# A fused decoder layer: the cross stage's maxima added by VectorE, two score tiles in one exp, outputs by halves, and a new table of priorities

## The reference

```python
x = _layernorm(x + self_attention(x))         # q, k, v: rope(x @ w.T) @ in_proj.T + b; softmax with causal mask
x = _layernorm(x + cross_attention(x, ctx))   # q = rope(x @ Wq.T + bq), k = rope(ctx @ Wk.T + bk), v = ctx @ Wv.T + bv
probs = softmax(x @ wg.T); top 2 of 8, weights normalised
out = sum over experts e of w_e * (silu(x @ w1[e].T) * (x @ w3[e].T)) @ w2[e].T
x = _layernorm(x + out)
```

## Time and profile before

| | us |
|---|---|
| median of 3 runs (249.85 to 252.05) | 249.91 |
| the profiled execution | 248.22 |
| its span, first to last instruction | 246.40 |
| PE busy (share of the span) | 232.7 (94%) |
| DVE busy | 186.0 (75%) |
| ACT busy | 161.3 (65%) |
| POOL busy | 89.1 (36%) |
| the chain of waits that ended last | PE 80%, DVE 10%, ACT 4%, issue 3%, DMA 2% |

### The profile page before, as it was taken

How to read it: one execution, slowest core, us unless ns; L and a number is a source line. 1 busy time by engine, 2 the same in 40 slices (tenths; PEclk the granted TensorE clock), 3 DMA queues, 4 the chain that set the end, 5 groups by cost and what they waited for, 6 DMA issues and landing times.

```text
span 246.4 us, 4685 instructions
## 1 busy us (share of the span) xinstructions
PE 232.7 (94%) x1438; PEld 164.7 (67%) x1438; DVE 186.0 (75%) x631; ACT 161.3 (65%) x332; POOL 89.1 (36%) x161
## 2 busy tenths in 40 slices
PE   7999999999999999999999999988899999999981
PEld 3456668666666776677765576553588878987860
DVE  5558987989879899986876898990399763348974
ACT  2488785889778779897898734747368765022234
POOL 9998547241432453355221211174011000470300
PEclk9999999999999999999999999999999999999998
DMA  6990002000003100000221000011311101010101
GB/s 237 340 330 3 1 1 85 3 1 4 0 0 117 56 1 3 1 0 3 81 87 60 32 1 3 0 53 58 106 32 44 45 21 54 25 53 11 39 7 43
DMA packets 10568, 12.57 MB, mean 51 GB/s; under 512 B 1200, under 2 KB 7728, under 8 KB 10416
## 3 DMA queue, kind: packets, MB, share of 16 engines
q1 hardware_dynamic: 9456, 10.43, 12.9%
q0 software_dynamic: 512, 1.05, 1.4%
q10 hardware_dynamic: 576, 0.79, 0.9%
HBM read 9.25 MB, written 3.01 MB: 50 GB/s over the span
## 4 chain that ended last, share of the span: by engine, by line
PE 80%; DVE 10%; ACT 4%; issue 3%; DMA 2%; DVEq 0%; ACTq 0%; SPq 0%
PE psB L1083 12%; PE psA L1054 12%; PE psO L1106 10%; PE psJ L952 3%; PE psJ L1186 3%; PE psJ L990 3%; PE psJ L953 3%; PE psJ L1067 2%; PE psA L1249 2%; PE psO L1111 2%; PE psO L982 2%; PE psJ L1065 2%; PE psA L1231 2%; PE psJ L997 1%; DMA xT<-xt_dram 1%
## 5 line engine op out<-in xcount | busy, mean ns | idle before, releaser
L1576 DVE CUSTOM_DVE_ANT_0 junk<-psA,c 128x128 bf16<-128x128 f32 (+3 forms) x128 | 55.7, 487 | 8.8 <-PE psA L1054 8.4
L1348 ACT ACTIVATE prob<-psB 128x512 f32<-128x512 f32 (+1 forms) x88 | 47.4, 558 | 13.6 <-PE psB L1083 11.8
L1083 PE MATMUL psB<-qb,kst 128*128 128x512 f32 (+3 forms) x128 | 38.0, 338 | 0.2 <-ACT prob_more L1348 0.2
L1054 PE MATMUL psA<-kst,qa 128*128 128x512 f32 (+1 forms) x88 | 36.6, 425 | 0.0
L1083 PEld LDWEIGHTS psB<-qb,kst 128*128 128x128 f32 x128 | 22.8, 189 | 11.4 <-issue 4.3
L1581 DVE TENSOR_REDUCE negm<-psA 128x3 f32<-128x462 f32 (+1 forms) x48 | 26.4, 579 | 4.5 <-PE psA L1054 3.9
L1348 ACT ACTIVATE prob_more<-psB 128x512 f32<-128x512 f32 (+1 forms) x48 | 24.5, 527 | 6.1 <-PE psB L1083 5.9
L1392 ACT ACTIVATE silu<-psA 128x512 f32<-128x512 f32 x16 | 9.6, 599 | 24.4 <-DVE hid L1739 18.0
L899 POOL TENSOR_SCALAR_AFFINE_SELECT prob<-prob 128x256 f32<-128x256 f32 x32 | 13.0, 408 | 31.3 <-ACT prob_more L1348 31.3
L1054 PEld LDWEIGHTS psA<-kst,qa 128*128 128x128 f32 x88 | 16.4, 188 | 6.0 <-issue 3.9
L1106 PE MATMUL psO<-prob_more,v 128*32 128x512 f32 (+3 forms) x128 | 20.3, 439 | 0.0
(11 more groups left out here) (198 smaller groups left out, 562.6 us busy)
## 6 DMA issues: line engine op xcount, KB each, us to landing
c<-w_dram SPq DMA_DIRECT2D x8, 256.0 KB, 2.6
w<-w_dram SPq DMA_DIRECT2D x1, 1024.0 KB, 4.7
xs_dram<-kst SPq DMA_DIRECT2D x1, 960.0 KB, 7.2
ys_dram<-ys SPq DMA_DIRECT2D x7, 128.0 KB, 1.8
rest<-xs_dram SPq DMA_DIRECT2D x3, 256.0 KB, 2.8
c<-c_dram SPq DMA_DIRECT2D x1, 666.0 KB, 8.5
xT<-xt_dram SPq DMA_DIRECT2D x2, 256.0 KB, 4.7
x_tok<-x_dram SPq DMA_DIRECT2D x1, 512.0 KB, 9.5
```

The source lines that it names most:

```text
L1054: last = nc.tensor.matmul(ps[:, c:c + heads * width].rearrange("p (n w) -> p n w", n=heads), qa[:, u % SLOTS, 128 * i:128 * i + 128], keys ...
L1083: last = nc.tensor.matmul(ps[:, c:c + S - 128 * kt], keys, qb[:, u % 2, 128 * kt:S], start=m == 0, stop=m == len(blocks) - 1, skip_group_c ...
L1348: nc.scalar.activation(dst, psB[n % SIZE["B"]][:, 0:cols], ACT.Exp, scale=SCALE).then_inc(b_done[n % SIZE["B"]], 1)
L1576: last = nc.vector.tensor_tensor_reduce(out=junk[:, p, cols], in0=psA[p][:, cols], in1=c32[:, C_MASK + S - width:C_MASK + S], scale=-1.0, ...
```

## The change

It has four parts.

1. In the cross stage (units 8 to 15, `max_by_dve`) MT no longer copies the q stack through the identity: PE only transposes the four blocks of `mpad` into the bank, and DVE adds `qa` to it on the way into `qb` (a new DVE item MT). ACT's copy is gone. The ring slot of `qa` is free only after DVE's addition.
2. In the self stage key tile 2 of two heads shares a bank (columns 0 and 256), and one exp of 512 columns takes both: 10 fills and 10 exps in a unit for 12.
3. The second pair of a batch row (p = 1, 3, 5, 7) is transposed and divided by halves (`turns`): OT becomes two jobs of two transposes, one reciprocal and two multiplications each on half the elements. ONT of half h waits for that half alone.
4. The table `EARLY` is another one, and the whole order with it. (Two waits are also written out more fully: DVE's OT waits for both ONT of the row before, and CQ waits for the low part too.)

```diff
+def max_by_dve(u):
+    st, b, g = unit(u)
+    return st == 1
 def b_fills(u):
     if unit(u)[0] == 0:
-        kinds = (((0, 0),), ((1, 0), (3, S - 128)), ((2, 0),))
-        return [tuple((kt, j, c) for kt, c in tiles) for tiles in kinds for j in range(G)]
+        kinds = (((0, 0),), ((1, 0), (3, S - 128)))
+        return [tuple((kt, j, c) for kt, c in tiles) for tiles in kinds for j in range(G)] + [((2, j, 0), (2, j + 1, 256)) for j in range(0, G, 2)]
+def turns(p):
+    return [("OT", (p, h)) for h in range(2)] if p % 2 else [("OT", (p,))]
...
-        add("MT", (u,), [("PE", 0.67), ("ACT", 0.5)], [("MP", (u,))],
+        add("MT", (u,), [("PE", 0.45), ("DVE", 0.69)] if max_by_dve(u) else [("PE", 0.67), ("ACT", 0.5)], [("MP", (u,))],
...
-            add("ONT", (st, b, h), [("PE", 0.24), ("ACT", 0.3)], [("OT", (p,))],
+            add("ONT", (st, b, h), [("PE", 0.24), ("ACT", 0.3)], [("OT", (p, h)), ("OT", (p - 1,))],
...
 EARLY = {
-    ('A', 11): 2, ('A', 13): 11, ('A', 14): -6, ('A', 7): -28, ('A', 8): 284, ('B', 1): 194, ('B', 13): 61, ('B', 6): 38,
+    ('A', 5): -39, ('A', 6): -17, ('A', 7): -199, ('B', 2): -11, ('B', 4): -19, ('B', 6): -55, ('B', 8): -30, ('CK',): -203,
...
                 elif kind == "MT":            # TensorE
-                    nc.tensor.matmul(ps[:, :], fr_id[:, :], qa[:, u % SLOTS, :], start=True, stop=False, skip_group_check=True)
+                    alone = max_by_dve(u)
+                    if not alone:
+                        nc.tensor.matmul(ps[:, :], fr_id[:, :], qa[:, u % SLOTS, :], start=True, stop=False, skip_group_check=True)
                     for i in range(QT):
-                        last = nc.tensor.matmul(ps[:, 128 * i:128 * i + 128], mpad[:, u % 2, i, :], fr_id[:, :], start=False,
-                                                stop=i == QT - 1, skip_group_check=True)
+                        last = nc.tensor.matmul(ps[:, 128 * i:128 * i + 128], mpad[:, u % 2, i, :], fr_id[:, :], start=alone,
+                                                stop=alone or i == QT - 1, skip_group_check=True)
...
+                elif kind == "MT":            # VectorE
+                    u, = args
+                    ps = bank(JOB[item])
+                    if u >= 2:
+                        dve.wait_ge(s_b, FILL["B"]["B", (u - 2, len(b_fills(u - 2)) - 1)] + 1)
+                    free(JOB[item], nc.vector.tensor_tensor(qb[:, u % 2, :], ps[:, :], qa[:, u % SLOTS, :].bitcast(FP32), ALU.add))
...
-                    nc.scalar.activation(dst, psB[n % SIZE["B"]][:, 0:cols], ACT.Exp, scale=SCALE).then_inc(b_done[n % SIZE["B"]], 1)
+                    nc.scalar.activation(dst, scores, ACT.Exp, scale=SCALE).then_inc(b_done[n % SIZE["B"]], 1)
...
-                    link(nc.vector.reciprocal(rec[:, p % 2, :], ps[:, :].rearrange("p (n c) -> p n c", c=V_AT)[:, :, HD]))
-                    sums = rec[:, p % 2, :].rearrange("p (i j h) -> p i j h", i=QT, j=G)
+                    link(nc.vector.reciprocal(rec[:, p % 2, at], ps[:, :].rearrange("p (n c) -> p n c", c=V_AT)[:, at, HD]))
+                    sums = rec[:, p % 2, at].rearrange("p (i j h) -> p i j h", i=n, j=G)
```

More of the change, by code:

```diff
@@ L108, in exps_of @@
     if unit(u)[0] == 0:
-        return {0: range(4), 1: range(4, 8), 3: range(4, 8), 2: range(8, 12)}[kt]
+        return {0: range(4), 1: range(4, 8), 3: range(4, 8), 2: range(8, 10)}[kt]
     return {0: range(4), 1: [4]}[kt]
@@ L184, in tasks @@
     row = lambda u: (u // NG // B, u // NG % B)
-    q_slot = lambda u: [(("MT", (u - SLOTS,)), 0)] if u >= SLOTS else []
+    q_slot = lambda u: [(("MT", (u - SLOTS,)), int(max_by_dve(u - SLOTS)))] if u >= SLOTS else []
     add("SET", (), [("POOL", 17.0)])
@@ L266, in tasks @@
         p = u // 2
-        add("POC", (p,), [("ACT", 0.49)], [last_pv(u)] + ([(("OT", (p - 1,)), 0)] if p else []))
-        add("OT", (p,), [("PE", 0.44), ("DVE", 0.8)], [("POC", (p,)), ("LOAD", (3,))],
-            [(1, ("ONT", row(u - NG) + (1,)))] if g == 1 and u >= NG else [])
+        add("POC", (p,), [("ACT", 0.49)], [last_pv(u)] + ([(turns(p - 1)[-1], 0)] if p else []))
+        for item in turns(p):
+            whole = len(item[1]) == 1
+            add("OT", item[1], [("PE", 0.44), ("DVE", 0.8)] if whole else [("PE", 0.24), ("DVE", 0.5)], [("POC", (p,)), ("LOAD", (3,))],
+                [(1, ("ONT", row(u - NG) + (1,)))] if g == 1 and u >= NG else [])
         if g < NG - 1:
@@ L1060, in _ @@
                     u, = args
-                    st, b, g = unit(u)
                     ps = bank(JOB[item])
@@ L1119, in _ @@
                     pe.wait_ge(s_po, p + 1)
-                    for i in range(QT):
+                    for i in range(QT) if len(args) == 1 else (2 * args[1], 2 * args[1] + 1):
                         last = nc.tensor.transpose(ps[:, 128 * i:128 * i + 128], po_sb[:, 128 * i:128 * i + 128], ident)
@@ L1297, in _ @@
                     u = unit_of(st, b, g)
-                    if u >= SLOTS:
+                    if u >= SLOTS and max_by_dve(u - SLOTS):
+                        job_done(act, "MT", u - SLOTS)
+                    elif u >= SLOTS:
                         job_filled(act, ("MT", (u - SLOTS,)))
@@ L1341, in _ @@
                     kt, j, _ = b_fills(u)[k][0]
-                    if st == 0:
-                        half, first = (prob, prob_more)[j // 2], j % 2 * 1280 + [0, 512, 1024][kt]
-                        cols = 256 if kt == 2 else 512
-                        dst = half[:, u % 2, first:first + cols]
-                    else:
-                        cols, dst = S, prob_at(u, kt, j)
-                    nc.scalar.activation(dst, psB[n % SIZE["B"]][:, 0:cols], ACT.Exp, scale=SCALE).then_inc(b_done[n % SIZE["B"]], 1)
+                    scores = psB[n % SIZE["B"]][:, :]
+                    if st == 0 and kt == 2:
+                        dst = (prob, prob_more)[j // 2][:, u % 2, :].rearrange("p (j c) -> p j c", j=2)[:, :, 1024:1280]
+                        scores = scores.rearrange("p (j c) -> p j c", j=2)
+                    elif st == 0:
+                        half, first = (prob, prob_more)[j // 2], j % 2 * 1280 + [0, 512][kt]
+                        dst = half[:, u % 2, first:first + S]
+                    else:
+                        dst = prob_at(u, kt, j)
+                    nc.scalar.activation(dst, scores, ACT.Exp, scale=SCALE).then_inc(b_done[n % SIZE["B"]], 1)
                 elif kind == "POC":
@@ L1352, in _ @@
                     if p:
-                        job_filled(act, ("OT", (p - 1,)))
+                        for other in turns(p - 1):
+                            job_filled(act, other)
                     nc.scalar.activation(po_sb[:, :], psO[:, :], ACT.Copy).then_inc(s_po, 1)
```

20 lines of the change are left out of this document (13 added, 7 removed), and 22 rows, old and new, of the table EARLY.

## The result

The changed kernel took 253.31 us (median of 4 runs, 252.55 to 255.02) beside 250.98 for the kernel before (median of 4, 249.85 to 252.13). The ratio is 1.0115, with a 95% interval from 1.0065 to 1.0165: slower by a little over 1%, where 249.5 was forecast. The profiled execution took 252.55, with a span of 250.8 (246.4 before) and a mean granted clock of 0.984 (0.997 before). That last pair is the first thing to see; the other three executions had 0.988, 0.974 and 0.984.

What follows compares the result with a forecast made beforehand. PE bounds the kernel up to 135 and in the R and F products, DVE in 141 to 160 and near the end. Terms -0.96 - 0.5 + 1.1 + 2.0 - 1.4 - 0.6 = -0.4 give 249.5, range 245.5 to 252.3.

Steps and rivals of the forecast that it cites:

- rival (d): TensorE's clock falls once in 141 to 160 as its waits move: +4, total 253; chance 4%.
- Step 1: MT of units 8 to 11: four identity copies go from PE's full stretch, DVE's additions cost nothing; -0.96.
- the mark: End of row 1's second CQ, 135.57 before, forecast at 137.2.
- Step 2: Joined exps of tile 2 win back part of the 2.3 stall at the context keys: -0.5, bounds 0 and -2.3.
- Step 3: At the start, MT of unit 0 comes at 26.6 with row 1's q projection still owed: +1.1.
- Steps 1 to 4 together: Up to row 1's second CQ: -0.96 - 0.5 + 1.1, and +2.0 for work moved ahead; 137.2 for 135.57.
- Step 5: CQ to first R1, paced by DVE: divisions 3.8, ranks 19.9 after the mark; 39.4 for 40.8, -1.4.
- What R1 still owed: PE work now behind the first R1: a fill, two bursts and the last OT, 2.5 in all.
- the two products: In the tail, the last R3 stands two products further back: 6 x 0.24 = 1.4.
- Step 6: Tail, last R3 to first FL: 29.8 for 30.6, with 11.6 of DVE's queue after YC; -0.6.
- (b): DVE bounds CQ mark to unit 15's scores if pair 5's divisions start less than 1 earlier: 251.5; 17%.
- within 1%: Whole kernel's time within 1% (2.5) of the kernel before, neither under 247.4 nor over 252.4: chance 0.56.

Runs made afterwards that it cites:

- e9: The changed kernel, unedited, run again on one chip with the kernel before: 249.64 us beside 247.79, ratio 1.0074.
- e10: The kernel before, unedited, run again on the same chip as e9: 247.79 us, twelve executions from 247.50 to 248.57.
- e4: The changed kernel with MT of units 8 to 15 back on identity copy and ACT: 249.25 us beside 247.85 for the kernel before, ratio 1.0068.
- e2: The kernel before's order with all three code edits (DVE additions, joined exps, halves): 250.83 us beside 247.85 for the kernel before, ratio 1.0118.
- e6: The kernel before's order with only DVE's additions for MT of units 8 to 15: 251.70 us beside 251.06, ratio 1.0039.
- e5: The kernel before's order with only the joined exps of key tile 2: 252.51 us beside 251.06, ratio 1.0038.
- e8: The kernel before without 13 fillers between 143 and 149, with the two fuller waits: 253.39 us beside 251.06, ratio 1.0059.
- e12: The changed kernel with 12 more fillers ahead of SQ of unit 12, at 139: 248.20 us beside 247.79 for the kernel before, ratio 1.004.
- e3: The changed kernel's order with the code of the kernel before: 256.14 us beside the kernel before, ratio 1.0321.
- e1: The changed kernel with 12 more fillers where TensorE waits around 158: 248.3 us beside 247.85 for the kernel before, ratio 1.002.

## Why the prediction was wrong

The pair on one chip with the clock full (e9 and e10; spans 246.9 and 246.8) tests the steps without the clock. Their rows, the kernel before first:

```profile
28.31 0.39 PE L1083 MATMUL psB<-qb,kst 128*128 128x512 f32 x1
...
134.84 1.03 PE L1150 MATMUL psJ<-xT,wx 128*128 128x256 f32 x4
...
176.70 0.49 PE L1231 MATMUL psA<-wp,xr_high 128*128 x1
```

and the changed kernel:

```profile
28.28 0.43 PE L1099 MATMUL psB<-qb,kst 128*128 128x512 f32 x1
...
135.64 1.06 PE L1167 MATMUL psJ<-xT,wx 128*128 128x256 f32 x4
...
174.26 0.49 PE L1248 MATMUL psA<-wp,xr_high 128*128 x1
...
227.39 1.13 DVE L1761 SCALAR_TENSOR_TENSOR z<-prob,gsm,x_tok 128x128 f32<-128x128 f32 x4
...
238.91 1.13 PE L1211 MATMUL psJ<-w,hid 128*128 128x128 f32 x8 [0.95 <-issue]
```

FL began at 238.83 in e10 and at 238.91 in e9: +0.1, where the sum said -0.4.

- **The step that failed is rival (d)'s chance, not a term.** I gave the clock 4% because it was 1.00 "through today's waits", and priced it at 253; 253.31 came. The sum had no term for it. The runs showed instead a clock of 0.50 for 7 us in the first trace, 2.5 on the path (e9), in nine of the changed kernel's fourteen executions. The price was near partly by luck: +4 was forecast for 6 us of TensorE's work at low clock, and 2.5 came for 7 us at 0.50. The median of 253.31 has a kernel before of 250.98 beside it, 1.1 above the 249.91 that the forecast started from. One profiled execution can't show how near a kernel stands to losing its clock, and my table had the sign of it: of the three times of before one was 252.05 beside 249.85 and 249.91. I took the median past it. The new order makes TensorE wait 1.59 ahead of SQ and 0.74 ahead of unit 14's scores, where the kernel before waited 0.41 and 0.39, and the new table's fillers stand ahead of neither. The prediction had TensorE wait for the divisions and the ranks, and did not ask what longer waits do to the clock.
- **Step 1** (-0.96): the addition costs 0.686, and it is hidden in the new order. Putting the copies back costs 0.7 at the mark (e4), so the term was an upper end. In the old order it isn't hidden (e2, e6).
- **Step 2** (-0.5, bound -2.3): the stall went from the chain altogether. The far bound was nearer.
- **Step 3** (+1.1): MT of unit 0 came at 27.00 (26.6 forecast), and at 26.73 beside 26.37 in the pair, but the first B is level there (28.28 and 28.31). The q projection was still owed.
- **Steps 1 to 4 together**: the mark moved by 136.70 - 135.87 = 0.83 in the pair, for 1.64. With the stall gone I should have seen about 1.8 less than forecast, and 0.8 is there; where the other 1.0 went isn't settled.
- **Step 5**: in the pair the divisions begin 4.6 after the mark, `place_u` ends at 20.7 and R1 begins at 37.6, for 3.8, 19.9 and 36.9. The walk of VectorE's queue from the divisions on held (16.1 both ways); only their start was forecast 0.8 too early, as SQ waited 1.59 for the queries.
- **What R1 still owed** (2.5) and the two products (1.4): 3.9 forecast, 4.4 measured, in the first pair of traces (212.90 - 176.98 = 35.9 for 31.5).
- **Step 6**: from YC to FL 238.91 - 227.39 = 11.5, for 11.6 counted. In the first trace of the changed kernel YC stood 1.2 later after the last R3 than in e9. The rows of POOL, which issues the gather, say where: after the last of its eight issues, here in the first trace and then in e9:

```profile
224.45 0.94 POOL L931 DMA_INDIRECT prob<-ys_dram,place_u  x1 [0.30 <-issue]
...
231.28 1.13 DVE L1761 SCALAR_TENSOR_TENSOR z<-prob,gsm,x_tok 128x128 f32<-128x128 f32 x4
```

```profile
221.73 0.94 POOL L931 DMA_INDIRECT prob<-ys_dram,place_u  x1 [0.30 <-issue]
```

From the end of that issue to YC it is 5.9 in the first trace and 4.7 in e9, as in all five others of the new order. In the old order it is 2.9 to 3.2 in before, e2 and e10, and 4.3 to 4.4 in all four of e5 to e8, whatever the edit or the clock. So the 1.2 goes with the chip and not with the change, and the first trace of the changed kernel seems to come from a chip like that of e5 to e8, the trace of before from one like the others. It may also be what stands behind the 1.69 between the profile of before and its median, which the prediction carried along unexplained.
- **(b)** did not decide: the divisions start 2.0 earlier after the mark, above its threshold of 1.

So at full clock the change costs 0.1 in the pair of profiles and 0.9 in the medians (248.65 for 247.79), inside the "within 1%" of the forecast, and the lost clock adds 2.5 in some executions: half of them on one chip, and all four of the first measurement. The ten executions of e12 at full clock, the same order with other fillers, have a median of 248.15, which is 0.4. Part of the difference is which execution was profiled: that of before in the pair was the longest of its twelve, 248.57. Where the rest lies isn't settled.

## What to carry to other kernels

- When a change moves an engine's waits, list the waits of TensorE that become longer, and see whether something without use stands in them. A single trace at full clock says nothing about the distance to the edge; the spread of the single times does, so read each execution's mean clock before its time. Within the group at full clock it says no more: on the chip of e9 the kernel before took 247.50 to 247.78 at 0.995 and 248.24 to 248.66 at 0.998 or more.
- Set two traces beside each other only if they come from one chip, or find a stretch that the change leaves alone and see that it is equal in both. Here the wait after the gather differed by 1.2 between chips.
- Edits and the order made for them must be tried together: here each alone was 3 and 7 us slower, and both together 0.9. A test of one part in the other's order tells what that part leans on, not what it is worth.
- A job cut in two takes two turns of its ring of buffers; count the ring's waits as well as the work.

## What the runs showed of the hardware

- TensorE's granted clock goes from 1.00 to 0.50 in one step, after waits of 0.74 and 0.73 (the changed kernel, e3) or about a microsecond in two parts (e8) beside a full VectorE, and after one of 1.36 with VectorE idle (e5). It comes back after some 3.5 us in e3 and e5, 7 in the changed kernel and 10 in e8. The same wait of 0.74 stands in e9's trace at a clock of 1.00 throughout.
- Over a whole execution a lost clock costs 2.5 in the changed kernel (e9), 2.1 in the kernel before (chip of e5 to e8) and 0.8 in e1. Whether it happens differs from execution to execution and from chip to chip, for the same instructions: none of 45 executions of the kernel before on one chip, at least 13 of 31 on another.
- Twelve matmuls of 256 columns in one earlier wait, 20 us ahead, were followed by two losses in twelve executions, for five of ten without; that is a sign, not a proof. With 22 in three waits it was none of twelve.
- From the last issue of an indirect gather to the first use of what it brought took 1.2 longer on one chip than on two others, in every kernel run there (4.3 to 4.4 for 2.9 to 3.2 in the old order). What holds it wasn't looked into.
